# Recurrent steps by token halves, and the final state's product shared by all tiles

## The chip, the cores and the metric

The kernel runs on one core of one Trainium2 chip. The metric is the device time of one execution in microseconds, the median of several. The engines are named as the profile names them: PE is TensorE (PEld its weight loads), ACT is ScalarE, DVE is VectorE, POOL is GpSimd and SP the engine that issues most DMAs.

## The reference, cut to what matters

Eight tiles `t` of 512 tokens with 128 features each pass linear attention (per tile alone), a first layer norm, a recurrence over the tiles, and a second layer norm. The recurrence is where the change lies: token `n` of tile `t` follows token `n` of tile `t - 1`, so tokens don't depend on one another, and only the state of the last tile enters the output.

```
x = layernorm(x + attention(x))                 # tile by tile
def step(c, xt):
    ft = sigmoid(xt @ wf.T + c @ uf.T + bf)
    it = sigmoid(xt @ wi.T + c @ ui.T + bi)
    gt = tanh(xt @ wc.T + c @ uc.T + bc)
    return ft * c + it * gt, None
c_final, _ = lax.scan(step, c0, x)              # over the 8 tiles
h = tanh(einsum('tbi,oi->tbo', x, wo) + c_final @ uo.T + bo)
x = layernorm(x + h)
```

The product `c_final @ uo.T + bo` is the same for all eight tiles.

## The kernel before

Everything stays on the chip. The constants are `T = 8` tiles, `N = 512` tokens and `D = 128` features; a tile has `C = 4` blocks of 128 tokens, and one PSUM bank holds one tile. There is no planner: each engine has its own program, whose order is written out by hand, and engines meet at semaphores. Each engine's queue runs in the order of its program.

The body runs in periods (`periods()`, L197). In period `n` tile `n + 1` has its keys and queries made (`k`), tile `n` its attention products (`a`), tile `n - 1` its attention end and first norm (`b`), and tile `n - 2` its recurrent step (`t`). A step on TensorE is nine products of 512 columns from x1 and nine from the state: weights and operands are each split in a high and a low part in fp32r, and three of the four products are made, for three gates (`gate_x_high` L362, `gate_x_low` L373, `gate_s` L394). ScalarE makes three tanh of a whole bank (`tanh` L545); VectorE makes the kept part (L701), the new part (L774) and the state (L781); ScalarE copies the state's high part (`s_hi`, L591); GpSimd makes the low part (`s_lo`, L276), and VectorE that of the last step (L735). The first norm's result is transposed (`x1_turned` L350), split by ScalarE (`x1_high` L564) and VectorE (`x1_low` L690), and kept as columns (`x1_whole` L568). Only for the last tile are the tanh of gate c, the new part and the state made in two halves.

The output is made in nine parts (`OUT_PARTS`, L148) of a tile each, tile 0 in two. `out_x` (L398) makes x1 times wo, block by block in fp32, and adds the bias; three of the parts come ahead of the last gates on TensorE. `out_s` (L429) adds the last state times uo, again for every block of every tile. Then ScalarE takes the tanh in place (L615), VectorE adds the residual (L790), makes statistics (L663) and variance (L669, L810), GpSimd makes the reciprocal root (L247) and the shift (L255), and of a unit's four blocks VectorE normalises one (L799) and ScalarE three (L557); SP stores the unit (L221). `UNITS` (L46) are seven tiles and the last tile in two halves. ScalarE makes the tanh of unit `u` before it normalises unit `u - ACT_AHEAD`, three earlier; on VectorE a residual stands one unit ahead of the statistics.

## Time and profile before

| | us |
|---|---|
| median of 3 runs | 106.99 |
| lowest, highest | 106.97, 107.19 |
| the profiled execution | 107.27 |
| its span, first to last instruction | 105.2 |

| engine | busy us | share of the span |
|---|---|---|
| TensorE | 92.5 | 88% |
| VectorE | 79.5 | 76% |
| ScalarE | 62.1 | 59% |
| GpSimd | 40.6 | 39% |

The profile comes from one execution, whose time is 2.1 us more than its span. Times inside it count from the span's start. A share of busy time is a mean over stages that have different limits, so the stages have to be read apart. "Chain" is the chain of work that ended last: for each piece the view goes back to what released it. In its rows a TensorE product is set down by its end; in the timeline its row begins where it starts and lasts until its result is written, so products overlap there.

### The profile page before, as it was taken

The page shows a single profiled execution, that of the slowest core. Times are in us where ns is not written, and L with a number is a line of the kernel's source. Part 1 is how long each engine was busy: PE and PEld are TensorE (multiplying, and loading weights), DVE is VectorE, ACT ScalarE, POOL GpSimd, SP SyncE. Part 2 cuts the span into 40 slices and gives each one's busy share as a digit, 9 for nine tenths or more (in the row PEclk, how much of TensorE's full clock was granted, in tenths as well). Part 3 has the DMA queues.
Part 4 walks back from the last instruction along what each step waited for, and adds up shares of the span by engine and source line. Part 5 has one row for each costly group of instructions (what it writes and reads, how often), then busy time and mean ns, then how long its engine had stood idle before and what let it go on. Part 6 is the DMA issues. An engine that isn't in the chain of part 4 may idle for free.

```text
span 105.2 us, 1758 instructions
## 1 busy us (share of the span) xinstructions
PE 92.5 (88%) x570; PEld 78.5 (75%) x570; DVE 79.5 (76%) x225; ACT 62.1 (59%) x115; POOL 40.6 (39%) x59
## 2 busy tenths in 40 slices
PE   6998999889999999999999999999999999991000
PEld 4878779469688968878887888898898899991000
DVE  3325398998999995898689589389592648999950
ACT  1326675349395684676659374374753735799731
POOL 2006277607247149009306604304300002786780
PEclk9999999999999999999999999999999999999855
DMA  1869994000000000000000000000000000034453
GB/s 44 284 250 406 387 386 176 6 0 3 0 0 0 0 0 0 9 0 0 0 0 6 0 0 0 0 0 0 3 0 6 0 0 0 0 142 161 179 211 108
DMA packets 4372, 7.28 MB, mean 69 GB/s; under 512 B 491, under 2 KB 1292, under 8 KB 4364
## 3 DMA queue, kind: packets, MB, share of 16 engines
q1 hardware_dynamic: 3932, 6.85, 17.7%
q10 hardware_dynamic: 432, 0.33, 1.1%
q8 instruction: 4, 0.07, 0.2%
q14 instruction: 4, 0.03, 0.1%
HBM read 5.08 MB, written 2.10 MB: 68 GB/s over the span
## 4 chain that ended last, share of the span: by engine, by line
PE 72%; DVE 18%; POOL 3%; ACT 3%; issue 2%; POOLq 0%; DVEq 0%; ACTq 0%
PE ps_ctx L326 7%; PE ps_k L307 7%; PE ps_ctx L346 6%; PE ps_q L317 5%; DVE stats L663 5%; DVE x L790 4%; PE ps_f L296 4%; PE ps_x L357 3%; POOL rstd L247 2%; DVE x L675 2%; PE ps_f L370 2%; PE ps_f L376 2%; PE ps_c L371 2%; PE ps_c L370 2%; PE ps_c L376 2%; PE ps_i L371 2%
## 5 line engine op out<-in xcount | busy, mean ns | idle before, releaser
L247 POOL TENSOR_TENSOR rstd<-var_eps,minus_half 128x4 f32<-128x4 f32 (+1 forms) x17 | 17.2, 1012 | 22.6 <-DVE var_eps L669 22.3
L276 POOL TENSOR_TENSOR s_lo<-s,s_hi 128x512 fp32r<-128x512 f32 x6 | 7.7, 1291 | 26.7 <-ACT s_hi L591 26.7
L663 DVE BATCH_NORM_STATS2 stats<-x 128x6 f32<-128x256 f32 x32 | 12.3, 425 | 0.3
L675 DVE TENSOR_SCALAR x<-x,stats,rstd 128x128 f32<-128x128 f32 x32 | 11.4, 420 | 0.0
L557 ACT ACTIVATE x<-x,shift,rstd 128x128 f32<-128x128 f32 x21 | 8.9, 480 | 3.6 <-POOL shift L255 3.6
L238 POOL TENSOR_TENSOR k_pair<-k_rows 128x256 f32<-128x256 f32 x8 | 6.3, 785 | 9.9 <-DVE k_rows L697 9.9
L566 ACT ACTIVATE x_hi<-ps_x 128x512 fp32r<-128x512 f32 x8 | 4.8, 597 | 8.6 <-PE ps_x L357 8.6
L326 PEld LDWEIGHTS ps_ctx<-k_rows,x_rows 128*128 128x128 f32 x64 | 8.1, 191 | 2.0 <-issue 1.6
L326 PE MATMUL ps_ctx<-k_rows,x_rows 128*128 128x128 f32 x64 | 8.6, 278 | 0.8 <-DVE x L686 0.5
L307 PE MATMUL ps_k<-wkq,x_cols 128*128 128x128 f32 x64 | 9.3, 293 | 0.0
L537 ACT ACTIVATE k_exp<-ps_k,minus_one 128x512 f32<-128x512 f32 x8 | 5.5, 686 | 6.2 <-PE ps_k L311 6.2
L686 DVE SCALAR_TENSOR_TENSOR x<-ps_ctx,z_inv,x_rows 128x128 f32<-128x128 f32 x32 | 9.0, 341 | 0.1
L346 PEld LDWEIGHTS ps_ctx<-kvo,q_cols 128*128 128x128 f32 x64 | 8.3, 191 | 1.0 <-issue 0.5
L307 PEld LDWEIGHTS ps_k<-wkq,x_cols 128*128 128x128 f32 x64 | 8.8, 209 | 0.2
L346 PE MATMUL ps_ctx<-kvo,q_cols 128*128 128x129 f32 x64 | 8.5, 276 | 0.0
L551 ACT ACTIVATE th_f<-ps_f,half_b 128x512 f32<-128x512 f32 x7 | 4.8, 690 | 5.7 <-PE ps_f L392 5.7
L317 PE MATMUL ps_q<-x_cols,wkq 128*128 128x512 f32 x16 | 8.2, 593 | 0.0
L721 DVE TENSOR_TENSOR kvo<-ps_ctx,eps_z 128x129 f32<-128x129 f32 x8 | 2.3, 293 | 7.5 <-PE ps_ctx L337 7.5
L707 DVE SCALAR_TENSOR_TENSOR keep<-th_f,s 128x512 f32<-128x512 f32 x7 | 4.8, 686 | 3.5 <-ACT th_f L551 3.5
L697 DVE SCALAR_TENSOR_TENSOR k_rows<-k_exp,ps_k 128x512 f32<-128x512 f32 x8 | 5.4, 679 | 1.8 <-ACT k_exp L537 1.8
L774 DVE SCALAR_TENSOR_TENSOR new<-th_i,th_c 128x512 f32<-128x512 f32 (+1 forms) x9 | 5.6, 628 | 1.6 <-ACT th_c L551 1.6
L551 ACT ACTIVATE th_i<-ps_i,half_b 128x512 f32<-128x512 f32 x7 | 4.8, 688 | 2.3 <-PE ps_i L392 2.3
(161 smaller groups left out, 242.2 us busy)
## 6 DMA issues: line engine op xcount, KB each, us to landing
x_cols<-xt SPq DMA_DIRECT2D x8, 256.0 KB, 7.0
x_rows<-x SPq DMA_DIRECT2D x8, 256.0 KB, 7.2
out<-x SPq DMA_DIRECT2D x7, 256.0 KB, 2.0
wgate<-w_gate SPq DMA_DIRECT2D x1, 384.0 KB, 6.7
out<-x SPq DMA_DIRECT2D x2, 128.0 KB, 1.8
wkq<-w_kq ACTq DMA_DIRECT2D x1, 131.0 KB, 3.4
wvo_in<-w_vo_in ACTq DMA_DIRECT2D x1, 128.0 KB, 3.3
wout<-w_out SPq DMA_DIRECT2D x1, 128.0 KB, 6.9
```

The costliest lines, as they stand in the source:

```text
L238: nc.gpsimd.tensor_tensor(k_pair[:], k_rows[:, a % 2, 0:C // 2], k_rows[:, a % 2, C // 2:C], ALU.add).then_inc(k_pair_ok, 1)
L247: nc.gpsimd.tensor_tensor(rstd[:, t, c0:c1], var_eps[:, t, c0:c1], minus_half[:, c0:c1], ALU.pow).then_inc(rstd_ok, 1)
L276: nc.gpsimd.tensor_tensor(s_lo[:, (t - 1) % 2], s[:, (t - 1) % 2].rearrange("p c d -> p (c d)"), s_hi[:, (t - 1) % 2].bitcast(F32), ALU.su ...
L307: nc.tensor.matmul(ps_k[:, c * D:(c + 1) * D], x_cols[:, a, c], wkq[:, WK_T * D:(WK_T + 1) * D], start=(c == 0), stop=False, skip_group_ch ...
L317: nc.tensor.matmul(ps_q[:], wkq[:, WQ_T * D:(WQ_T + 1) * D], x_cols[:, a].rearrange("p c d -> p (c d)"), start=True, stop=True).then_inc(q ...
L326: mm = nc.tensor.matmul(small[:, 0:D], x_rows[:, a, c], k_rows[:, a % 2, c], start=(c == 0), stop=(c == C - 1))
L346: mm = nc.tensor.matmul(ctx_view[:, c // 2, c % 2], q_cols[:, b % 2, c], kvo[:, b % 2], start=True, stop=True, skip_group_check=True)
L551: nc.scalar.activation(out_tile[:, part], ps[:, part], ACT.Tanh, bias=bias, scale=scale).then_inc(ok, 1)
L557: nc.scalar.activation(x1[:, t, c], x1[:, t, c], ACT.Identity, bias=shift[:, t, c:c + 1], scale=rstd[:, T + t, c:c + 1]).then_inc(y2_act_o ...
L663: st = nc.vector.bn_stats(stats[:, t, c:c + 2].rearrange("p c m -> p (c m)"), tile[:, c:c + 2].rearrange("p c d -> p d c"))
L675: nc.vector.tensor_scalar(x1[:, b, c], x1[:, b, c], mean_of(b, c), rstd[:, b, c:c + 1], ALU.subtract, ALU.mult).then_inc(x1_ok, 1)
L686: ins = nc.vector.scalar_tensor_tensor(x1[:, b, c], ctx_view[:, c // 2, c % 2, 0:D], z_inv[:, b % 2, c:c + 1], x_rows[:, b, c, 0:D], ALU.m ...
```

## The change

Steps 0 to 3 are made as before, but steps 4 to 7 are made for tokens 0 to 255 and for tokens 256 to 511 apart, in an order written out in `STEPS`: 4a, 5a, 4b, 6a, 7a, 5b, 6b, 7b (a the first half, b the second), so that with steps 0 to 3 there are twelve entries. The periods end with n = 6, and what follows is written out on each engine. An output unit is now two blocks of two tiles: four units of the first halves, three of the second halves, and the second halves of tiles 6 and 7 alone. For each half the state's product with uo and the bias is made once (`out_g`), split in a high part (ScalarE, `g_high`) and a low part (VectorE, `g_low`), and added to seven of the nine units by two fp32r products with the identity (`add_g`); units 0 and 4 (`DIRECT`) still make the product themselves. The x1 parts have eight buffers instead of two. The low part of the state is made by GpSimd for entries up to 7 and by VectorE for entries 9 and 10. In the tail ScalarE makes the tanh of unit `u` and then normalises unit `u - 1`; VectorE makes residual, statistics and variance of one unit in a row, then its block of the unit before.

```diff
-ACT_AHEAD = 3
-UNITS = [(t, 0, C) for t in range(T - 1)] + [(T - 1, 0, C // 2), (T - 1, C // 2, C)]
-DVE_NORM = [1, 1, 1, 1, 1, 1, 2, 2, 1]
+H = C // 2
+STEPS = [(0, 0, C), (1, 0, C), (2, 0, C), (3, 0, C), (4, 0, H), (5, 0, H), (4, H, C), (6, 0, H),
+         (7, 0, H), (5, H, C), (6, H, C), (7, H, C)]
+FULL_PERIODS = 7
+UNITS = [(0, 2, 0), (2, 2, 0), (4, 2, 0), (6, 2, 0), (0, 2, H), (2, 2, H), (4, 2, H), (6, 1, H), (7, 1, H)]
+DVE_NORM = [1, 1, 1, 1, 1, 1, 1, 1, 1]
+DIRECT = (0, 4)
...
+        g_bank = [ps_x1[:, 0:H * D], ps_q[:, 0:H * D]]
+        unit_bank = [ps_k[:], ps_q[:], ps_ctx[:, 0, :], ps_ctx[:, 1, :], ps_x1[:], ps_k[:], ps_f[:], ps_i[:], ps_c[:]]
...
+            state_low(4)
+            reciprocal_root(6)
+            reciprocal_root(7)
+            state_low(5)
+            state_low(6)
+            state_low(7)
+            for u in range(len(UNITS)):
+                second_root(u)
                 second_shift(u)
...
+            def gate_s(g, k):
+
+                ps, _, done = gates[g]
+                u, last, part = GATES + g, (STEPS[k][0] - 1) % 2, columns(k)
+                if k == 1:
                     pe.wait_ge(split_s_lo, 1)
+                pe.wait_ge(shi_ok[step_before(k)], 1)
+                nc.tensor.matmul(ps[:, part], wgate_hi[:, u], s_hi[:, last, part], start=False, stop=False,
+                                 skip_group_check=True)
...
+            def out_g(h):
+
+                ps = g_bank[h]
+                if h == 0:
                     pe.wait_ge(x1c_ok, T)
+                else:
                     pe.wait_ge(w_ok, 2)
+                pe.wait_ge(uo_ok, 1)
+                pe.wait_ge(s_ok, len(STEPS) if h else STEPS.index((T - 1, 0, H)) + 1)
+                for j in range(H):
+                    nc.tensor.matmul(ps[:, j * D:(j + 1) * D], s[:, (T - 1) % 2, h * H + j], uo_half[:],
+                                     start=(j == 0), stop=False, skip_group_check=True)
+                nc.tensor.matmul(ps, ones_r[:], row_parts[:, BOUT_ROW].unsqueeze(1).to_broadcast([D, H, D]),
+                                 start=False, stop=True, skip_group_check=True).then_inc(g_mm, 1)
+
+            def add_g(u):
+
+                ps, nt, h = unit_bank[u], UNITS[u][1], UNITS[u][2] // H
+                if u == 1:
+                    pe.wait_ge(ident_r_ok, 1)
+                pe.wait_ge(g_hi_ok, h + 1)
+                nc.tensor.matmul(ps[:, 0:nt * H * D], ident_r[:],
+                                 g_hi[:, h].unsqueeze(1).to_broadcast([D, nt, H * D]),
                                  start=False, stop=False, skip_group_check=True)
...
+                pe.wait_ge(g_lo_ok, h + 1)
+                nc.tensor.matmul(ps[:, 0:nt * H * D], ident_r[:],
+                                 g_lo[:, h].unsqueeze(1).to_broadcast([D, nt, H * D]),
+                                 start=False, stop=True, skip_group_check=True).then_inc(out_mm, 1)
...
+            gates_x(5)
+            keys_x(7)
+            gate_s(0, 5)
+            key_values(7)
+            gate_s(1, 5)
+            gate_s(2, 5)
+            context(7)
+            gates_x(6)
+            gates_s(6)
+            x1_turned(6)
+
+            out_x(0)
+            gates_x(7)
+            gates_s(7)
+            x1_turned(7)
             out_x(1)
-            out_x(5)
-            for o in range(len(OUT_PARTS)):
-                if o >= 6:
-                    out_x(o)
-                out_s(o)
+
+            gates_x(8)
+            gates_s(8)
+            gates_x(9)
+            gates_s(9)
+            out_g(0)
+            out_s(0)
+            add_g(1)
+            gates_x(10)
+            out_x(2)
+            gates_s(10)
+            add_g(2)
+            gates_x(11)
+            out_x(3)
+            gates_s(11)
+            add_g(3)
+            out_x(4)
+            out_s(4)
+            out_g(1)
+            for u in range(5, len(UNITS)):
+                out_x(u)
+                add_g(u)
...
+            act.wait_ge(ident_ok, 1)
+            nc.scalar.activation(ident_r[:], ident[:], ACT.Copy).then_inc(ident_r_ok, 1)
...
+            state_high(4)
+            x1_whole(5)
+            xk_copy(7)
+            gates_tanh(5)
+            gates_tanh(6)
+            x1_high(6)
+
+            state_high(5)
+            x1_whole(6)
+            gates_tanh(7)
+            state_high(6)
+            x1_high(7)
+
+            state_high(7)
+            x1_whole(7)
+            gates_tanh(8)
+            gates_tanh(9)
+            g_high(0)
+            out_tanh(0)
+            state_high(9)
+            out_tanh(1)
+            gates_tanh(10)
+            normalise(0)
+            state_high(10)
+            out_tanh(2)
+            normalise(1)
+            gates_tanh(11)
+            out_tanh(3)
+            normalise(2)
+            out_tanh(4)
+            g_high(1)
+            normalise(3)
+            for u in range(5, len(UNITS)):
+                out_tanh(u)
+                normalise(u - 1)
+            normalise(len(UNITS) - 1)
...
+            attention_end(6)
+            key_values(7)
+            normalise(6)
+            kept_state(5)
+            new_state(5)
+            reciprocal_z(7)
+            next_state(5)
+            attention_end(7)
+            step(6)
+            x1_low(6)
+
+            normalise(7)
+            step(7)
+            x1_low(7)
...
+            step(8)
+            step(9)
+            g_low(0)
             second_residual(0)
+            second_statistics(0)
+            second_variance(0)
+            state_low(9)
             second_residual(1)
+            second_statistics(1)
+            second_variance(1)
+            step(10)
+            second_normalise(0)
+            state_low(10)
+            second_residual(2)
+            second_statistics(2)
+            second_variance(2)
+            second_normalise(1)
+            step(11)
+            second_residual(3)
+            second_statistics(3)
+            second_variance(3)
+            second_normalise(2)
+            second_residual(4)
+            g_low(1)
+            second_statistics(4)
+            second_variance(4)
+            second_normalise(3)
+            for u in range(5, len(UNITS)):
+                second_residual(u)
                 second_statistics(u)
                 second_variance(u)
+                second_normalise(u - 1)
             second_normalise(len(UNITS) - 1)
```

## Rows read from the trace of the kernel before

**Rows 1.** The chain's share of the span by engine, from the page.

```profile
PE 72%; DVE 18%; POOL 3%; ACT 3%; issue 2%; POOLq 0%; DVEq 0%; ACTq 0%
```

**Rows 2.** Busy time by stage: stretch, length, busy us (x instructions) by engine, clock.

```profile
62.00:70.30 8.30, 8.09 (x53) 7.03 (x52) 6.38 (x18) 4.13 (x7) 2.31 (x2) 1.00 0.00 0
70.30:78.00 7.70, 7.70 (x50) 6.77 (x49) 6.46 (x18) 4.46 (x7) 2.30 (x2) 1.00 0.00 1
78.00:84.40 6.40, 6.24 (x35) 5.10 (x34) 3.34 (x8) 3.42 (x6) 0.00 (x0) 1.00 0.01 3
...
91.50:105.20 13.70, 3.66 (x31) 3.39 (x29) 9.88 (x40) 9.16 (x22) 8.33 (x15) 0.77 0.42 154
```

**Rows 3.** The chain in order of time: start, duration, engine, tile, line, instructions.

```profile
62.00 0.45 PE ps_x L357 x4
62.47 0.61 ACT x_hi L566
63.21 0.47 PE ps_f L370
63.68 0.24 PE ps_f L371
...
70.31 0.89 PE ps_q L423 x8
...
84.41 0.68 PE ps_k L437 x4
...
102.50 0.49 ACT x L557
```

**Rows 4.** Instruction groups by form: shapes and count, then busy us, mean ns, idle before.

```profile
L238 POOL TENSOR_TENSOR k_pair<-k_rows 128x256 f32<-128x256 f32 x8 | 6.3, 785 | 9.9 <-DVE k_rows L697 9.9
...
L551 ACT ACTIVATE th_c<-ps_c,wkq 128x256 f32<-128x256 f32 x2 | 0.8, 471 | 0.0
...
L781 DVE SCALAR_TENSOR_TENSOR s<-keep,new 128x256 f32<-128x256 f32 x2 | 0.8, 416 | 0.0
```

**Rows 5.** The timeline from 82 to 84.6 us: start, duration, engine, line, operation.

```profile
82.39 0.60 PE L423 MATMUL ps_f<-wout,x_cols 128*128 128x128 f32 x4
...
82.72 0.19 PEld L425 LDWEIGHTS ps_f<-row_parts,ones_r 128*128 128x128 f32 x1
82.75 0.36 PE L425 MATMUL ps_f<-row_parts,ones_r 128*128 128x256 f32 x1
...
82.95 1.06 PE L423 MATMUL ps_x<-wout,x_cols 128*128 128x128 f32 x8
...
83.84 0.75 DVE L781 SCALAR_TENSOR_TENSOR s<-keep,new 128x256 f32<-128x256 f32 x2
```

**Rows 6.** The timeline of the tail, from 86.4 us.

```profile
86.47 0.58 ACT L615 ACTIVATE ps_q<-ps_q 128x512 f32<-128x512 f32 x1 [0.53 <-PE ps_q L437]
87.08 0.69 DVE L790 TENSOR_TENSOR x<-x,ps_q 128x512 f32<-128x512 f32 x1 [0.69 <-ACT ps_q L615]
...
88.48 0.17 DVE L669 TENSOR_SCALAR var_eps<-stats 128x4 f32<-128x4 f32 x1
...
88.73 1.01 POOL L247 TENSOR_TENSOR rstd<-var_eps,minus_half 128x4 f32<-128x4 f32 x1 [13.69 <-DVE var_eps L669]
...
89.88 0.20 POOL L255 TENSOR_TENSOR shift<-minus_mean,rstd 128x4 f32<-128x4 f32 x1
...
90.11 1.26 ACT L557 ACTIVATE x<-x,shift,rstd 128x128 f32<-128x128 f32 x3 [1.27 <-POOL shift L255]
...
94.61 0.57 ACT L615 ACTIVATE ps_i<-ps_i 128x512 f32<-128x512 f32 x1
...
95.12 1.24 ACT L557 ACTIVATE x<-x,shift,rstd 128x128 f32<-128x128 f32 x3
...
96.27 0.57 ACT L615 ACTIVATE ps_c<-ps_c 128x512 f32<-128x512 f32 x1
...
101.23 0.80 POOL L247 TENSOR_TENSOR rstd<-var_eps,minus_half 128x2 f32<-128x2 f32 x1
```

More of the change, by code:

```diff
@@ L187, in rows_of, with columns, step_before, state @@
             return dram[t].rearrange("(p c) d -> p c d", c=C)
-        def halves(cut):
-            return [slice(0, N // 2), slice(N // 2, N)] if cut else [slice(0, N)]
-        def act_norms(units):
-            return sum(c1 - c0 - mine for (_, c0, c1), mine in zip(UNITS[:units], DVE_NORM))
-        def periods():
-            def inside(v):
-                return v if 0 <= v < T else None
-            for n in range(T + 2):
-                yield inside(n + 1), inside(n), inside(n - 1), inside(n - 2)
+        def columns(k):
+            _, c0, c1 = STEPS[k]
+            return slice(c0 * D, c1 * D)
+        def step_before(k):
+            t, c0, _ = STEPS[k]
+            return max(j for j in range(k) if STEPS[j][0] == t - 1 and STEPS[j][1] <= c0 < STEPS[j][2])
+        def state(t):
+            return s[:, t % 2].rearrange("p c d -> p (c d)")
+        def blocks(u):
+            t0, nt, c0 = UNITS[u]
+            return [(t, c) for t in range(t0, t0 + nt) for c in (c0, c0 + 1)]
+        def part_of(tile, u, t_first=0):
+            t0, nt, c0 = UNITS[u]
+            return tile[:, t_first + t0:t_first + t0 + nt, c0:c0 + H]
+        def periods():
+            for n in range(FULL_PERIODS):
+                yield n + 1, n, n - 1 if n >= 1 else None, n - 2 if n >= 2 else None
+        def act_norms(units):
+            return sum(len(blocks(u)) - DVE_NORM[u] for u in range(units))
         @block.sync
@@ new lines, in out_x @@
+                for j, (t, c) in enumerate(blocks(u)):
+                    nc.tensor.matmul(ps[:, j * D:(j + 1) * D], x1_cols[:, t, c], wout[:, 0],
+                                     start=(j == 0), stop=False, skip_group_check=True)
+                n = len(blocks(u))
+                if u not in DIRECT:
+                    return
+                nc.tensor.matmul(ps[:, 0:n * D], ones_r[:], row_parts[:, BOUT_ROW].unsqueeze(1).to_broadcast([D, n, D]),
+                                 start=False, stop=False, skip_group_check=True)
@@ new lines, in out_s @@
+            def out_s(u):
+                ps = unit_bank[u]
+                if u == 0:
+                    pe.wait_ge(uo_ok, 1)
+                pe.wait_ge(s_ok, len(STEPS) if UNITS[u][2] else STEPS.index((T - 1, 0, H)) + 1)
+                n = len(blocks(u))
+                for j, (_, c) in enumerate(blocks(u)):
+                    mm = nc.tensor.matmul(ps[:, j * D:(j + 1) * D], s[:, (T - 1) % 2, c], uo_half[:],
+                                          start=False, stop=(j == n - 1), skip_group_check=True)
+                mm.then_inc(out_mm, 1)
@@ L494, in _ @@
                 if t is not None:
-                    for g in range(GATES):
-                        gate_x_high(g, t)
-                    for g in range(GATES):
-                        gate_x_low(g, t)
-                    if a is not None:
-                        keys_x(a)
+                    gates_x(t)
+                    keys_x(a)
                     gate_s(0, t)
-                if a is not None:
-                    key_values(a)
+                key_values(a)
                 if a == 1:
@@ L767, in _ @@
                 if t is not None:
-                    if t != T - 2:
-                        kept_state(t)
-                    dve.wait_ge(i_ok, t + 1)
-                    parts = halves(t == T - 1)
-                    for h, part in enumerate(parts):
-                        dve.wait_ge(c_ok, t + 1 + h)
-                        nc.vector.scalar_tensor_tensor(new[:, part], th_i[:, part], 1.0, th_c[:, part],
-                                                       ALU.add, ALU.mult).then_inc(new_ok, 1)
@@ L776, in _ @@
-                    if a is not None:
-                        reciprocal_z(a)
-                    dve.wait_ge(keep_ok, t + 1)
-                    for h, part in enumerate(parts):
-                        dve.wait_ge(new_ok, t + 1 + h)
-                        nc.vector.scalar_tensor_tensor(s[:, t % 2].rearrange("p c d -> p (c d)")[:, part], keep[:, part], 0.5,
-                                                       new[:, part], ALU.mult, ALU.add).then_inc(s_ok, 1)
-                if b is not None and b >= 1:
-                    x1_low(b)
```

371 lines of the change are left out of this document (196 added, 175 removed).

## The prediction

> **What bounds the kernel now.** Read the chain by engine first: TensorE holds 72% of it, VectorE 18% [rows 1]. That mean hides two stages, which the busy time by stage parts [rows 2]. Up to 84.4 us TensorE is nearly full (8.09 of 8.30, 7.70 of 7.70, 6.24 of 6.40 us) and everything else waits for it. Behind it the second normalisation runs: TensorE falls to 3.66 us of the last 13.7, and a unit of four blocks moves through ScalarE, VectorE, GpSimd and ScalarE again. The last state is whole at 84.6 us (L781) [rows 5]; from there the chain has 18.4 us to the end of the last ScalarE instruction (103.0 us) [rows 3], and 2.2 more to the end of the span for the last store. So two numbers decide: when the last state stands, and how long the tail behind it is. The change shortens the second (four of nine units come before) and puts work ahead of the first.
>
> **The price of one instruction.** A 512-column gate product takes 0.234 us of TensorE (0.23 and 0.24 in the chain) [rows 3]. A 256-column one isn't in the gates of before, but its like stands once between fp32 products: from the first start (82.39) to the next behind it (82.95) is 0.56 us [rows 5], and the four before it take half of the 0.89 of eight [rows 3], so it takes 0.11. I take 0.117, half of 0.234; the far end is 0.19, the recorded time of a weight load [rows 5], if loads stopped hiding behind so short a product; below 0.107 nothing points. A 256-wide operation takes 0.42 us on VectorE (0.34 where two follow each other), 0.47 (0.37) for ScalarE's tanh, about 0.78 on GpSimd (L238, the nearest row) [rows 4, 5]. From the end of one to the start of the next: 0.04 from TensorE to ScalarE, 0.03 to 0.1 between ScalarE and VectorE and inside VectorE. A TensorE that stood still gives its first 512-column product 0.60 us after the signal (x_hi ends at 63.08, product at 63.68) [rows 3]; for 256 columns 0.49.
>
> **The change, by parts.** (1) Eight half steps for four whole ones: 144 products of 0.117 for 72 of 0.234, nothing on TensorE. On ScalarE and VectorE two halves cost 0.06 to 0.15 us more than a whole, for about 28 pairs some 3 us, mostly beside TensorE; where not, it is in the walk. (2) Product with uo: before, 32 blocks of 0.223 and biases worth eight of 0.235, 9.0 us. After: 12 blocks (2.7), biases 0.7, additions of two products by the identity for seven units (2.8): 6.2 us. The 2.8 us saved lie on an engine that runs ahead in the tail, and are worth nothing there. (3) Order: what else stands on TensorE ahead of the last gate. Before, 10 blocks of x1 times wo with bias, 2.8 us; after, 16 blocks with one bias (3.8), g of the first half (0.56), unit 0's product (0.89), two additions (0.94), 6.2 us. So 3.4 us more ahead of the last state. (4) Copies of g, high and low, 0.4 each on ScalarE and VectorE, twice. (5) One copy of the identity at the start, in ScalarE's wait for the first x·k product: nothing; 0.4 at most if that cover is gone. (6) Eight x1 parts instead of two: no time. (7) State_low of entries 9 and 10 goes to VectorE, queued behind a unit's variance: in the walk. (8) Stores on SP: nine as before, four of them before the last state; nothing else stands on that queue by then, and the last is half a tile as before.
>
> **Walk to the last state.** I laid each engine's new order along these prices, from 53.6 us, where period 6 begins and nothing differs yet. Period 6 has only half of step 4 and ends at 60.6 where it ended at 62.45 [rows 3]. From there TensorE has 24.0 us of work to the end of the last gate (seven half steps of 2.11; attention 2.2; transposes 0.9; the 6.2 of part 3): 84.65 if nothing stops it. It is stopped:
> - 1.0 at gates_x(5), for x_hi of tile 5, which ends at 61.24 (0.6 at that place before).
> - 0.26 at keys_x(7) and key_values(7): less work stands between them and what they wait for.
> - 1.1 at the low products of gates_x(7). VectorE ends s of entry 5 at 67.46, then attention_end(7) to 69.4 (residual 1.1, statistics 0.8), step(6) with its dependent state to 70.7, and only then x1_low(6), 71.34. TensorE is there at 70.6; first low product at 71.83.
> - 0.46 at gates_x(8): x1_high(7) stands on ScalarE behind the three tanh of entry 7 and state_high(6), and ends at 74.53. 0.2 at gates_s(8), for state_low(7) on GpSimd.
> - 0.6 at add_g(1): g is made at 79.87, copied high to 80.3, low on VectorE to 81.25.
> - 0.3 at gates_s(11): state_high(10) stands behind normalise(0) on ScalarE and ends at 86.9, state_low(10) on VectorE at 87.4.
> The sum is 3.95 us: the last gate is ready at 88.6. Its three tanh wait on ScalarE for normalise(1), to 88.5, and the last ends at 89.74, not 89.1. New part (0.10 + 0.42) and state (0.11 + 0.42): 90.8 us, against 84.6.
>
> **Walk of the tail.** One unit, from its rows [rows 6]: tanh to residual 0.61, residual to variance 1.40, variance to root 0.25, root to shift 1.15, shift to ScalarE's normalise 0.23, whose three blocks hold ScalarE 1.15. Before, a residual stands one unit ahead of its statistics; now the statistics wait for their own residual, 0.11 more. So from a unit's tanh to where its normalise lets ScalarE go is 4.90 us. Before, ScalarE had three units of tanh ahead of a normalise, and VectorE set the pace, 1.66 us a unit (tanh at 94.61 and 96.27) [rows 6]. The new order is tanh(u), normalise(u-1), tanh(u+1), normalise(u), so tanh(u+2) stands behind normalise(u): two units per 4.90 us, 2.45 each, with ScalarE idle for the shift. From the last state: unit 4's product and its signal 1.26 (the first four took 0.68 [rows 3]); tanh(4) to tanh(6) 4.90 + 0.25 for g_low(1) between; tanh(6) to tanh(8) 4.90; the last half unit 3.3 (0.4 to its residual, 0.9 to its variance, 0.25 to the root, 1.27 from root to normalise and 0.49 for it, as the last of before [rows 3, 6]); the store 2.2. That is 16.8, against 20.6 before: 3.8 gained.
>
> So the span is 90.8 + 16.8 = 107.6, which is 2.4 over 105.2. The profiled execution took 107.27 us: 109.7. The median of the runs stands 0.28 below it: 109.4 us.
>
> ScalarE keeps its written order in the rows (tanh 94.61, normalise 95.12, tanh 96.27) [rows 6]. The Trainium skill says the same, "TensorE: Matmul & The Clock Gate", section "Architectural detail: the array is 16× 32×32, not 1× 128×128": ScalarE's and VectorE's queues are strict first in, first out. It speaks against this change; without it rival (b) would hold.
>
> **Rivals.** (a) Most of TensorE's stops aren't there, since the halves cover each other better than my walk has it. For: the work alone ends at 84.65, and VectorE has 1.2 to 3 us free in each stage up to 84.4 [rows 2]. Against: each stop is an instruction behind others in its own queue. If those at gates_x(7), gates_x(8), add_g(1) and gates_s(11) and the late tanh go (3.1), the state stands at 87.7, the span is 104.5, the time 106.3; with half of the rest gone too, 105. Below 88.4 for the state the change is faster than before; that is the point from which it decides. 105.7, faster. (b) ScalarE's order costs nothing in the tail and VectorE paces it, 1.8 a unit and 1.15 for each of the two last halves: the last residual starts at 99.6 and not at 102.5, 106.5. Only if normalise is ready much sooner than the rows have it. (c) The narrow products don't hide their weight loads: 0.19 for 0.117, 144 of them, up to 10 us, of which the stops hide up to 3: 114 to 119. Against it is the 0.11 measured once; but that one had fp32 neighbours. (d) The change doesn't do what it says: nothing for it, the first half's units do come before the last state in every queue.
>
> **How the numbers follow.** The walk 0.67 (its own range 107.6 to 111.3: 0.2 on each of ten waits, 0.7 on the tail), (a) 0.20, (b) 0.06, (c) 0.07. The range, 105.8 to 111.3, leaves out (c) and about half of (a). A measurement of this kernel tells 0.2% (0.2 us) from no change. (a) and most of (b) are faster: 0.24. The same 0.04, slower 0.72.
>
> **What the profile of after would show.** Right: the last state near 90.8; TensorE idle about 1 us for x_lo ahead of the low products of gates_x(7); in the tail every second tanh 4.9 us apart and ScalarE waiting for GpSimd's shift; narrow products 0.117 apart. Wrong: the last state before 88.4, tanh of full units 1.8 us apart, or narrow products at 0.13 and more. The likeliest error is a wait put on the wrong engine between 70 and 88 us.

## The result, and the profile after

| | before | after |
|---|---|---|
| median, us | 106.98 | 109.72 |
| lowest, highest | 106.46, 107.19 | 109.29, 110.38 |
| the profiled execution | 107.27 | 109.29 |
| its span | 105.2 | 107.5 |

The ratio of after to before is 1.027, with a 95% interval of 1.021 to 1.033. In a second comparison, beside the experiments, it was 1.031 (1.026 to 1.037). The change makes the kernel 2.7 to 3.1% slower.

The chain by engine (page of after): TensorE has 58% where it had 72%, VectorE 23%, and ScalarE 9% where it had 3% [rows 1].

```profile
PE 58%; DVE 23%; ACT 9%; issue 4%; POOL 3%; POOLq 0%; DVEq 0%; ACTq 0%
```

Busy time by stage of after (stretch, length, then busy us of PE, PEld, DVE, ACT, POOL, and the granted clock). The third stretch ends with the last state, the fourth is the tail:

```profile
60.50:68.60 8.10, 7.95 (x65) 7.71 (x66) 7.01 (x26) 4.08 (x10) 1.75 (x2) 1.00 0.01 2
...
68.60:79.00 10.40, 9.62 (x73) 8.81 (x73) 6.38 (x17) 5.97 (x15) 3.27 (x4) 1.00 0.01 2
...
79.00:90.45 11.45, 10.58 (x81) 9.61 (x80) 10.11 (x30) 8.45 (x21) 4.13 (x6) 1.00 0.10 33
...
90.45:105.30 14.85, 6.06 (x45) 5.42 (x45) 10.90 (x37) 9.63 (x23) 7.37 (x13) 0.81 0.32 109
```

TensorE is no longer nearly full ahead of the last state: 9.62 of 10.40 us and 10.58 of 11.45, against 7.70 of 7.70 [rows 2]. VectorE is busy for 10.11 of the 11.45 us ahead of it.

Executions differ by up to 1 us in where the first periods stand. So I measure from the start of the state of step 3, the last one that all kernels here share, to the end of the last state (**head**), and from there to the end of the span (**tail**).

| kernel | step 3's state starts | last state ends | head | tail |
|---|---|---|---|---|
| before | 53.90 | 84.59 | 30.7 | 20.6 |
| after | 52.95 | 90.45 | 37.5 | 17.05 |
| after, second time | 53.86 | 91.31 | 37.45 | 17.0 |

The head is 6.8 us longer and the tail 3.6 us shorter: 3.25 us, of which the execution shown gave back 0.95 by starting its periods earlier.

The timeline of after at the low products of gates_x(7), at the first products of gates_x(8) and gates_x(9), at add_g(1), and at the last state (start, duration, engine, line, operation):

```profile
69.82 0.68 DVE L834 TENSOR_TENSOR x_lo<-ps_x,x_hi 128x512 fp32r<-128x512 f32 x1
...
70.56 0.39 PE L420 MATMUL ps_f<-x_lo,wgate_hi 128*128 128x256 f32 x1 [0.48 <-DVE x_lo L834]
...
72.52 1.06 PE L474 MATMUL ps_q<-wout,x_cols 128*128 128x128 f32 x8
...
72.97 0.60 ACT L683 ACTIVATE x_hi<-ps_x 128x512 fp32r<-128x512 f32 x1
...
73.72 0.36 PE L411 MATMUL ps_f<-x_hi,wgate_hi 128*128 128x256 f32 x1
...
75.92 0.47 ACT L650 ACTIVATE th_f<-ps_f,half_b 128x256 f32<-128x256 f32 x1 [0.51 <-PE ps_f L443]
...
76.44 0.38 PE L411 MATMUL ps_f<-x_hi,wgate_hi 128*128 128x256 f32 x1
...
76.81 0.39 PE L411 MATMUL ps_i<-x_hi,wgate_hi 128*128 128x256 f32 x1
...
80.61 0.42 DVE L961 TENSOR_TENSOR g_lo<-ps_x,g_hi 128x256 fp32r<-128x256 f32 x1
...
81.08 0.51 PE L519 MATMUL ps_q<-g_lo,ident_r 128*128 128x512 f32 x1 [0.29 <-DVE g_lo L961]
...
88.94 0.46 ACT L650 ACTIVATE th_c<-ps_c,wkq 128x256 f32<-128x256 f32 x1
...
89.11 0.42 DVE L850 SCALAR_TENSOR_TENSOR keep<-th_f,s 128x256 f32<-128x256 f32 x1
...
89.50 0.43 DVE L857 SCALAR_TENSOR_TENSOR new<-th_i,th_c 128x256 f32<-128x256 f32 x1
...
90.03 0.42 DVE L864 SCALAR_TENSOR_TENSOR s<-keep,new 128x256 f32<-128x256 f32 x1
```

TensorE waits for x_lo (0.48 us by the record, 0.75 in lost products) and for g's low part. At gates_x(8) it waits for x_hi of tile 7, though the row names no releaser: x_hi ends at 73.57, the product starts at 73.72, and that is 1.20 us after the eight products of out_x(1) started, where 0.82 us stand between two such starts elsewhere in after (82.48 and 83.30). So 0.4 us is lost there. In gates_x(9) there is a wait that no bullet of the walk has: a gate has one bank, and its next products wait until ScalarE has read the last ones (th_f ends at 76.39, the product starts at 76.44). That makes the three pairs 0.37 us apart for 0.24 (76.44, 76.81 and 77.17).

ScalarE's timeline of the tail of after:

```profile
91.72 0.57 ACT L669 ACTIVATE ps_x<-ps_x 128x512 f32<-128x512 f32 x1
...
93.63 1.26 ACT L674 ACTIVATE x<-x,shift,rstd 128x128 f32<-128x128 f32 x3 [0.97 <-POOL shift L287]
...
94.80 0.57 ACT L669 ACTIVATE ps_k<-ps_k 128x512 f32<-128x512 f32 x1
...
95.80 1.26 ACT L674 ACTIVATE x<-x,shift,rstd 128x128 f32<-128x128 f32 x3 [0.43 <-POOL shift L287]
...
96.96 0.57 ACT L669 ACTIVATE ps_f<-ps_f 128x512 f32<-128x512 f32 x1
...
98.66 1.26 ACT L674 ACTIVATE x<-x,shift,rstd 128x128 f32<-128x128 f32 x3 [1.12 <-POOL shift L287]
...
99.82 0.36 ACT L669 ACTIVATE ps_i<-ps_i 128x256 f32<-128x256 f32 x1
...
100.82 1.26 ACT L674 ACTIVATE x<-x,shift,rstd 128x128 f32<-128x128 f32 x3 [0.63 <-POOL shift L287]
...
101.98 0.36 ACT L669 ACTIVATE ps_c<-ps_c 128x256 f32<-128x256 f32 x1
```

The first row is the tanh of unit 4. From 94.80 on each tanh starts as a normalise ends. Tanh of units 4, 6 and 8 stand at 91.72, 96.96 and 101.98, and those of units 5 and 7 at 94.80 and 99.82: two units in 5.0 to 5.2 us. Between tanh and normalise ScalarE waits for GpSimd's shift (1.12 us ahead of 98.66).

### The profile page after: what moved, and what is told of

The parts are those of the page before. It is cut to its first block, busy times and chain, and to the rows that moved or that the text cites. A ratio compares the mean times of both kernels' runs of the same rounds, so it can differ in the third digit from the quotient of the medians.

```text
span 107.5 us, 1913 instructions
## 1 busy us (share of the span) xinstructions
PE 91.6 (85%) x611; PEld 78.8 (73%) x611; DVE 83.3 (77%) x236; ACT 65.2 (61%) x134; POOL 41.8 (39%) x61
## 4 chain that ended last, share of the span: by engine, by line
PE 58%; DVE 23%; ACT 9%; issue 4%; POOL 3%; POOLq 0%; DVEq 0%; ACTq 0%
PE ps_ctx L366 7%; PE ps_k L347 6%; PE ps_ctx L386 5%; PE ps_q L357 5%; ACT x L674 4%; PE ps_f L336 3%; DVE stats L974 3%; DVE x L817 3%; DVE x L966 3%; POOL rstd L280 3%; DVE s L864 2%; PE ps_x L397 2%; PE ps_ctx L376 2%; PE ps_f L420 2%; DVE new L857 2%
## 5 line engine op out<-in xcount | busy, mean ns | idle before, releaser
L293 POOL TENSOR_TENSOR s_lo<-s,s_hi 128x512 fp32r<-128x512 f32 (+1 forms) x8 | 8.1, 1010 | 23.2 <-ACT s_hi L660 23.2
L280 POOL TENSOR_TENSOR rstd<-var_eps,minus_half 128x4 f32<-128x4 f32 (+1 forms) x9 | 9.5, 1054 | 16.2 <-DVE var_eps L982 16.2
L674 ACT ACTIVATE x<-x,shift,rstd 128x128 f32<-128x128 f32 x23 | 9.8, 485 | 5.8 <-POOL shift L287 5.8
L275 POOL TENSOR_TENSOR rstd<-var_eps,minus_half 128x4 f32<-128x4 f32 x8 | 8.7, 1084 | 11.6 <-DVE var_eps L811 11.3
L650 ACT ACTIVATE th_f<-ps_f,half_b 128x256 f32<-128x256 f32 (+1 forms) x11 | 5.9, 532 | 7.3 <-PE ps_f L443 7.1
L347 PE MATMUL ps_k<-wkq,x_cols 128*128 128x128 f32 x64 | 8.4, 275 | 0.0
L850 DVE SCALAR_TENSOR_TENSOR keep<-th_f,s 128x256 f32<-128x256 f32 (+1 forms) x11 | 5.4, 490 | 3.0 <-ACT th_f L650 3.0
L650 ACT ACTIVATE th_i<-ps_i,half_b 128x256 f32<-128x256 f32 (+1 forms) x11 | 5.8, 528 | 2.7 <-PE ps_i L443 2.7
L857 DVE SCALAR_TENSOR_TENSOR new<-th_i,th_c 128x256 f32<-128x256 f32 (+1 forms) x12 | 6.1, 511 | 1.7 <-ACT th_c L650 1.7
L864 DVE SCALAR_TENSOR_TENSOR s<-keep,new 128x256 f32<-128x256 f32 (+1 forms) x12 | 6.5, 542 | 0.7
```

The costliest lines, as they stand in the source:

```text
L275: nc.gpsimd.tensor_tensor(rstd[:, b], var_eps[:, b], minus_half[:], ALU.pow).then_inc(rstd_ok, 1)
L280: nc.gpsimd.tensor_tensor(part_of(rstd, u, T), part_of(var_eps, u, T), minus_half[:, 0:nt * H].rearrange("p (t c) -> p t c", c=H), ALU.pow ...
L347: nc.tensor.matmul(ps_k[:, c * D:(c + 1) * D], x_cols[:, a, c], wkq[:, WK_T * D:(WK_T + 1) * D], start=(c == 0), stop=False, skip_group_ch ...
L650: nc.scalar.activation(out_tile[:, part], ps[:, part], ACT.Tanh, bias=bias, scale=scale).then_inc(ok, 1)
L674: nc.scalar.activation(x1[:, t, c], x1[:, t, c], ACT.Identity, bias=shift[:, t, c:c + 1], scale=rstd[:, T + t, c:c + 1]).then_inc(y2_act_o ...
L857: nc.vector.scalar_tensor_tensor(new[:, part], th_i[:, part], 1.0, th_c[:, part], ALU.add, ALU.mult).then_inc(new_ok, 1)
```

## The experiments

The ratio is to runs of the kernel before on the same chip. Head and tail are as above.

| kernel | us | ratio (95%) | head | tail |
|---|---|---|---|---|
| after again | 109.72 | 1.031 (1.026 to 1.037) | 37.45 | 17.0 |
| e1, tanh two units ahead | 106.52 | 1.003 (0.999 to 1.007) | 37.5 | 14.4 |
| e2, no shared product | 108.84 | 1.020 (1.014 to 1.026) | 37.0 | 16.8 |
| e3, before with shared product | 106.95 | 1.005 (1.001 to 1.009) | 30.6 | 21.5 |
| e4, before with ACT_AHEAD 2 | 111.20 | 1.041 (1.035 to 1.047) | 30.7 | 25.4 |
| e5, queue order | 109.17 | 1.026 (1.022 to 1.031) | 37.2 | 17.1 |
| e6, e1 and e5 | 106.54 | 1.002 (0.999 to 1.005) | 37.2 | 14.35 |
| e7, e6 and VectorE's tail | 106.52 | 1.003 (1.000 to 1.006) | 37.1 | 14.2 |
| e8, e1 with units 2, 3 behind | 108.60 | 1.018 (1.013 to 1.023) | 36.9 | 16.7 |
| e9, e7 with VectorE freed | 105.77 | 0.992 (0.988 to 0.995) | 36.4 | 14.2 |
| e10, e9 with norms moved | 105.84 | 0.993 (0.990 to 0.996) | 36.4 | 14.5 |
| e11, e1 with all units behind | 110.70 | 1.039 (1.030 to 1.048) | 35.1 | 20.4 |

The kernel before had medians of 106.32 to 106.51 us beside them.

**The changed kernel again**, unedited, as the measure for the others:

> The changed kernel as it is, as the base for the three beside it on the same chip: 2.7% over the kernel before, the last state at 90.2 to 90.5 us of the span.

Measured: 109.72 us, 1.031 (1.026 to 1.037), head and tail as in the first execution to 0.1 us. The last state ends at 91.31 and not at 90.2 to 90.5, since the periods of this execution stand 0.9 us later.

### The tail: ScalarE's order

**e1**, on the changed kernel:

```diff
             out_tanh(4)
             g_high(1)
-            normalise(3)
             for u in range(5, len(UNITS)):
                 out_tanh(u)
-                normalise(u - 1)
+                normalise(u - 2)
+            normalise(len(UNITS) - 2)
             normalise(len(UNITS) - 1)
```

> The changed kernel, with only ScalarE's order in the tail altered: tanh(5) to tanh(8) each stand ahead of normalise(3) to normalise(6), that is, tanh runs two units ahead of normalise and not one. Theory 1 (the tail is paced by tanh(u+2) standing behind normalise(u), 2.5 us a unit): the pace falls to VectorE's 1.8 us a unit, the last unit's residual starts near 99.6 and not at 102.4, the time is about 2.8 us shorter, 106.9 (106.2 to 107.6). The last state stays at 90.4. Rival (the tail is paced by VectorE or by GpSimd's root and shift, ScalarE's order only follows): within 0.5 us of the changed kernel, 109.2 to 109.8.

Measured: 106.52 us, 1.003. The head is the same to 0.1 us, the tail 2.7 us shorter. The timeline of e1 at ScalarE's tanh and VectorE's residuals:

```profile
93.83 0.58 ACT L669 ACTIVATE ps_k<-ps_k 128x512 f32<-128x512 f32 x1 [1.28 <-PE ps_k L519]
...
94.44 0.69 DVE L966 TENSOR_TENSOR x<-x,ps_k 128x512 f32<-128x512 f32 x1
...
95.48 0.58 ACT L669 ACTIVATE ps_f<-ps_f 128x512 f32<-128x512 f32 x1
...
96.37 0.68 DVE L966 TENSOR_TENSOR x<-x,ps_f 128x512 f32<-128x512 f32 x1
...
97.14 0.37 ACT L669 ACTIVATE ps_i<-ps_i 128x256 f32<-128x256 f32 x1
...
98.28 0.41 DVE L966 TENSOR_TENSOR x<-x,ps_i 128x256 f32<-128x256 f32 x1
```

Tanh of units 5, 6 and 7 are now 1.65 us apart, for 2.5 in after, and VectorE paces: its residuals stand 1.92 us apart (94.44, 96.37, 98.28), with its other work between them. The pace was expected at 1.8. Theory 1 is shown, its rival is out.

**e4**, on the kernel before, where the same loop is made by one number:

```diff
-ACT_AHEAD = 3
+ACT_AHEAD = 2
```

> The kernel before, with ACT_AHEAD 2 in place of 3: tanh runs two units ahead of normalise; there a residual stands one unit ahead of its statistics, so this makes the same loop as the changed kernel's (tanh(u+3) behind normalise(u), whose statistics need tanh(u+1)): two units per 4.8 us. Theory 1: from tanh of tile 3 on, 2.4 us a unit for 1.66; about 4.6 us slower, 111.6 (110.8 to 112.4). Rival (VectorE paces whatever ScalarE's order): within 0.5 us of before.

Measured: 111.20 us, 1.041, 4.9 us over the median beside it, where 4.6 were expected. ScalarE's timeline of e4:

```profile
90.78 0.57 ACT L615 ACTIVATE ps_ctx<-ps_ctx 128x512 f32<-128x512 f32 x1
...
92.45 0.57 ACT L615 ACTIVATE ps_x<-ps_x 128x512 f32<-128x512 f32 x1
...
94.53 1.26 ACT L557 ACTIVATE x<-x,shift,rstd 128x128 f32<-128x128 f32 x3 [1.51 <-POOL shift L255]
...
95.70 0.57 ACT L615 ACTIVATE ps_f<-ps_f 128x512 f32<-128x512 f32 x1
```

Two tanh 1.67 us apart, then 3.25: two units in 4.92 us, with ScalarE idle 1.51 us for the shift ahead of 94.53. The order alone makes that wait, in either kernel.

### The shared product

**e2**, on the changed kernel:

```diff
-DIRECT = (0, 4)
+DIRECT = tuple(range(9))
...
-            out_g(0)
             out_s(0)
-            add_g(1)
+            out_s(1)
...
-                add_g(u)
+                out_s(u)
```

> The changed kernel without the shared product: every unit makes its own product with uo and its bias, so g, its two copies and the identity products are gone; halves and order stay. Theory 1 (the shared product saves TensorE time where it is not needed): ahead of the last state TensorE has 0.75 us more work but does not wait about 0.5 us for the low part of g, in the tail 0.25 us between residual and statistics go: 109.4, within 0.4 of the changed kernel. Rival (the shared product carries the change, and the loss would be larger without it): the last state comes 0.8 us later and the tail is TensorE's, 110.5 or more. Rival 2 (the waits for g are what costs): faster by over 0.5 us.

Measured: 108.84, 1.020 (1.014 to 1.026), where after has 1.027 and 1.031: 0.7 to 1.1% under it. The head is 0.5 us shorter and the tail 0.2. Expected was no change within 0.4, which failed; rival 2 (faster by over 0.5 us) fits better. But e2 takes away the waits for g and the copies of g on ScalarE and VectorE together, so it is not shown which of them costs. The interval of e2 overlaps that of the first comparison of after (1.021 to 1.033) and ends where that of the second begins (1.026), so the size is not settled.

**e3**, on the kernel before (tiles 3 to 7 by identity products from one g of 512 columns):

```diff
+                if o == 4:
+                    out_g()
+                    out_x(6)
...
+                if o >= 4:
+                    add_g(o)
+                else:
+                    out_s(o)
```

> The kernel before, with only the shared product: whole steps, old units, but for tiles 3 to 7 the product with uo and the bias is made once (512 columns, bank of tile 7), split and added by identity products. TensorE has about 2.1 us less work. Theory 1 (worth nothing, since VectorE paces that tail): VectorE has 0.69 us more, and tile 3's product waits for the low part of g until about 90.5: 0.7 to 1.0 us slower, 107.8. Rival (TensorE's saving counts): faster than before by 0.5 us or more.

Measured: 106.95, 1.005 (1.001 to 1.009), 0.6 us over before where 0.7 to 1.0 was expected. Counted from the state of step 3, TensorE's last product ends 1.15 us sooner, and nothing comes of it: g's low part keeps tile 3's tanh back to 89.44, and VectorE has 0.69 us more. The head is 0.1 us shorter since a bias product of tile 3 left it. The shared product is no gain in either kernel.

### Ahead of the last state

**e5**, on the changed kernel, order only:

```diff
             attention_end(7)
-            step(6)
             x1_low(6)
+            step(6)
...
             gates_tanh(7)
-            state_high(6)
             x1_high(7)
+            state_high(6)
...
             out_s(0)
-            add_g(1)
             gates_x(10)
+            add_g(1)
...
-            normalise(1)
             gates_tanh(11)
             out_tanh(3)
-            normalise(2)
+            normalise(1)
             out_tanh(4)
             g_high(1)
+            normalise(2)
             normalise(3)
```

> The changed kernel with the order in the queues altered ahead of the last state, nothing added or removed: x1_low(6) ahead of step(6) on VectorE; x1_high(7) ahead of state_high(6) and the tanh of entry 11 and of unit 3 ahead of normalise(1), and tanh(4) ahead of normalise(2), on ScalarE; add_g(1) behind gates_x(10) on TensorE. The tail's order from unit 5 on stays. Theory 1 (the late last state is made of single instructions that stand behind others): the stop at gates_x(7) loses 0.5 to 0.9 us, that at gates_x(8) 0.4, at add_g(1) 0.3, and the tanh of entry 11 come 0.5 sooner; some of it comes back elsewhere: last state 1.5 us earlier, 88.9, and 1.5 us off the changed kernel's time (1.2 to 2.0). Rival (TensorE and the recurrence's own chain fill that time, the stops only show their slack): under 0.5 us.

Measured: 109.17, 0.55 us under the changed kernel beside it, the head 0.3 us shorter. Theory 1 wanted 1.2 to 2.0 us and falls for its size; the head fits the rival's bound of 0.5, the time is just over it. The stops were there, and changing the order at them gave little, because the ones looked at here had another wait behind them. The timeline of e5, at gates_x(7) and at the last state:

```profile
70.23 0.83 POOL L293 TENSOR_TENSOR s_lo<-s,s_hi 128x256 fp32r<-128x256 f32 x1
...
70.38 0.96 DVE L857 SCALAR_TENSOR_TENSOR new<-th_i,th_c 128x256 f32<-128x256 f32 x1
...
71.78 1.11 DVE L817 TENSOR_SCALAR x<-x,stats,rstd 128x128 f32<-128x128 f32 x4
...
88.56 0.47 ACT L650 ACTIVATE th_c<-ps_c,wkq 128x256 f32<-128x256 f32 x1
...
89.69 0.41 DVE L857 SCALAR_TENSOR_TENSOR new<-th_i,th_c 128x256 f32<-128x256 f32 x1
```

With x1_low(6) first, step(6) meets GpSimd's state_low(5) (its new part takes 0.96 us), normalise(7) ends at 72.9, and the transposes of tile 7 wait where the low products had waited: they start 0.84 us ahead of out_x(1) (72.27 and 73.11), for 0.44 in after (72.08 and 72.52). TensorE's stop has moved by some instructions. At the end the last tanh of entry 11 ends at 89.03, but the kept part starts at 89.35 and the new part at 89.69, behind unit 2's residual, statistics and variance on VectorE. In after tanh and VectorE's queue came free within 0.1 us of one another: th_c ends at 89.40, and the new part starts at 89.50, behind a kept part that starts at 89.11. So the earlier tanh of e5 gives nothing by itself.

**e6**, e5's order with e1's:

> The queue order of e5 and tanh two units ahead of normalise as in e1. If the two causes are apart (one ahead of the last state, one behind it), their gains add: 1.5 + 2.7 = 4.2 us off the changed kernel, 1.4% under the kernel before (0.980 to 0.991). If both free the same time: no more than the larger of the two, about the kernel before.

Measured: 106.54, 1.002 (0.999 to 1.005), outside the expected 0.980 to 0.991. By head and tail the gains add (0.3 and 2.7 us), but there was only 0.3 us of the first. In the time that 0.3 can't be told from e1's 1.003.

**e7**, e6 with VectorE's order in the tail:

```diff
-            second_normalise(2)
             second_residual(4)
             g_low(1)
+            second_normalise(2)
             second_statistics(4)
             second_variance(4)
-            second_normalise(3)
             for u in range(5, len(UNITS)):
                 second_residual(u)
+                second_normalise(u - 2)
                 second_statistics(u)
                 second_variance(u)
-                second_normalise(u - 1)
+            second_normalise(len(UNITS) - 2)
             second_normalise(len(UNITS) - 1)
```

> e6, and on VectorE in the tail normalise(u-2) stands between residual(u) and statistics(u), so that statistics don't wait for their own residual and normalise never waits for the root. Theory 1 (VectorE paces this tail once ScalarE doesn't, 1.92 us a unit in e1): 0.1 us a unit for five units, 0.4 to 0.5 us under e6. Rival (the pace is then TensorE's or the latency of the last unit): the same as e6.

Measured: 106.52, 1.003, the tail 0.1 us shorter where 0.4 to 0.5 was expected: within the noise of e6. The pace on VectorE fell from 1.92 to 1.81 us a unit, and the last residual stands 0.3 us nearer to the last state than in e1 (9.0 and 9.3 us behind its end), but half of that is lost again: the last unit's statistics now stand behind a block of the unit before (0.59 us from residual to statistics for 0.45).

**e8**, on e1, units 2 and 3 behind the last gates in every queue (TensorE's shown):

```diff
             gates_x(10)
-            out_x(2)
             gates_s(10)
-            add_g(2)
             gates_x(11)
-            out_x(3)
             gates_s(11)
+            out_x(2)
+            add_g(2)
+            out_x(3)
             add_g(3)
```

> The kernel of e1, with units 2 and 3 (out_x, add_g and all that follows on ScalarE and VectorE) moved behind the last gates in every queue; compare it with e1. Theory 1 (work put ahead of the last gate costs its own length there): 2.25 us of products leave TensorE's queue there and the last state comes 2.2 us earlier. Theory 2 (that work fills time in which the half steps would wait for one another): with it gone TensorE waits for the low part of the state, and the last state comes 1.0 us earlier at most (28.9 us behind the state of step 4's first half, for 29.9), while VectorE gets two more units behind it: 0.5 to 1.5 us slower than e1. Theory 1 with VectorE's pace of 1.8 a unit: about e1, within 0.5.

Measured: 108.60, 1.018, 1.6 us over e1 by the two ratios, 0.1 over theory 2's range. For 2.25 us of products taken away the head is 0.6 us shorter, and the tail is 2.3 us longer. TensorE's timeline of e8 shows where the rest went:

```profile
83.76 0.39 PE L443 MATMUL ps_f<-s_lo,wgate_hi 128*128 128x256 f32 x1 [0.49 <-DVE s_lo L875]
...
87.08 0.39 PE L438 MATMUL ps_f<-s_hi,wgate_hi 128*128 128x256 f32 x1 [0.77 <-ACT s_hi L660]
```

It stands idle for the low part and then for the high part of the state (1.26 us in all), and the first products of gates_x(11) wait for their banks, as those of gates_x(9) do (0.36 us a pair from 84.72).

**e11**, on e1, g and units 0 to 3 behind:

```diff
             gates_s(9)
-            out_g(0)
-            out_s(0)
-            add_g(1)
             gates_x(10)
-            out_x(2)
             gates_s(10)
-            add_g(2)
             gates_x(11)
-            out_x(3)
             gates_s(11)
+            out_g(0)
+            out_s(0)
+            add_g(1)
+            out_x(2)
+            add_g(2)
+            out_x(3)
             add_g(3)
```

> The kernel of e1, with g of the first half and units 0 to 3 all moved behind the last gates, in every queue; only x1 times wo of units 0 and 1 stays ahead. It measures what the half steps cost alone. 4.9 us of products and additions leave TensorE's queue ahead of the last gate, 4.0 us of unit work VectorE's. Theory 2 (the last steps 6b and 7b stand alone, and one half step alone needs about 3.65 us from state to state, as 7b in e8): the last state 27.5 us behind the state of step 4's first half, for 29.9 in e1, that is 2.4 earlier for 4.9 us of work; nine units behind it at 1.9 us: 111.5 to 112.5. Theory 1 (work ahead of the last gate costs its length): the state 4.5 to 5 us earlier, 109.5 to 110.5.

Measured: the last state starts 27.46 us behind that of step 4's first half (29.9 in e1), as theory 2 had it; the time, 110.70 (1.039), lies between the two ranges and doesn't decide: 0.8 us under theory 2's, whose tail was costed too long, and 0.2 over theory 1's. The timeline of e11:

```profile
83.95 0.42 DVE L864 SCALAR_TENSOR_TENSOR s<-keep,new 128x256 f32<-128x256 f32 x1
...
84.41 0.42 ACT L660 ACTIVATE s_hi<-s 128x256 fp32r<-128x256 f32 x1 [1.09 <-DVE s L864]
...
84.85 0.43 DVE L875 TENSOR_TENSOR s_lo<-s,s_hi 128x256 fp32r<-128x256 f32 x1 [0.48 <-ACT s_hi L660]
...
84.87 0.39 PE L438 MATMUL ps_f<-s_hi,wgate_hi 128*128 128x256 f32 x1 [0.65 <-ACT s_hi L660]
...
87.06 0.43 DVE L857 SCALAR_TENSOR_TENSOR new<-th_i,th_c 128x256 f32<-128x256 f32 x1 [0.37 <-ACT th_c L650]
...
87.59 0.43 DVE L864 SCALAR_TENSOR_TENSOR s<-keep,new 128x256 f32<-128x256 f32 x1
```

From state to state one half step alone takes 3.64 us (83.95 to 87.59): 0.46 until the high part is begun, 0.44 more until the low part and the first product, the nine products, then tanh, new part and state. The nine products start over 1.3 us of it; the rest of the way is other engines'. The work ahead of the last gate had cost 2.4 us. Its products are 4.2 us by the prices of part (3) (g 0.56, unit 0's product 0.89, two additions 0.94, eight blocks 1.78); the expectation's 4.9 is more than they add up to.

And e11 answers what the halves cost without g and the units. On TensorE its head has the same gate products as before and 0.8 us less of other work (8 blocks with one bias, 2.0 us, for 10 with theirs, 2.8), and is 35.1 us for 30.7: **4.4 us for steps 4 to 7 by halves**, in this order of the queues. The other 2.4 us of the 6.8 are the g product and units 0 to 3. How much of the 4.4 another order would give back was not tried on e11; on the kernel with all its work, the orders of e5 and e9 took 1.1 us off the head.

**e9**, e7 with VectorE freed between the steps:

```diff
             state_low(7)
+            state_low(9)
             for u in range(len(UNITS)):
...
             second_variance(0)
-            state_low(9)
...
             step(10)
-            second_normalise(0)
-            state_low(10)
             second_residual(2)
+            state_low(10)
             second_statistics(2)
             second_variance(2)
+            second_normalise(0)
             second_normalise(1)
...
             gates_tanh(10)
-            normalise(0)
-            state_high(10)
             out_tanh(2)
+            state_high(10)
+            normalise(0)
```

> The kernel of e7, with VectorE relieved from 82 to 90 us: state_low(9) goes to GpSimd; tanh of unit 2 stands ahead of state_high(10) and normalise(0) behind it on ScalarE; residual(2) stands ahead of state_low(10) on VectorE, so that it does not idle there. Theory 1 (from g on the last state is paced by VectorE's queue, which has units 0 to 2 between the steps): last state 0.4 to 0.8 us earlier than in e7 (29.56 behind the state of step 4's first half), and as much off the time: 1.0 to 1.5% better than e7 at best, 0.992 to 0.998 of the kernel before. Rival (TensorE's queue paces it): the last state within 0.1 of e7.

Measured: 105.77, 0.992 (0.988 to 0.995), the head 0.8 us shorter than e7's. The timeline of e9, behind the state of entry 9:

```profile
80.27 0.43 DVE L865 SCALAR_TENSOR_TENSOR s<-keep,new 128x256 f32<-128x256 f32 x1
...
81.58 0.73 POOL L293 TENSOR_TENSOR s_lo<-s,s_hi 128x256 fp32r<-128x256 f32 x1 [6.12 <-ACT s_hi L661]
```

The low part starts 1.31 us behind that state; in e7, behind unit 0's variance on VectorE, it started 2.61 us behind (80.98 and 83.59). At entry 11 the kept part starts 0.34 us behind the end of its tanh, for 1.05 in e7. So from g on the last state was held up by VectorE's queue, which had units 0 to 2 between the steps. The three edits were made together, and what each gives is not shown; ScalarE's copy of the high part of entry 10's state stands 0.46 us behind the state in both. This version is faster than both kernels, by 0.7 us (0.8%) against the one before, a small gain but clear of 1 by its interval.

**e10**, e9 with one block of units 2 and 4 moved to ScalarE:

```diff
-DVE_NORM = [1, 1, 1, 1, 1, 1, 1, 1, 1]
+DVE_NORM = [1, 1, 0, 1, 0, 1, 1, 1, 1]
```

> The kernel of e9, with VectorE's block of units 2 and 4 normalised by ScalarE (four blocks there, none on VectorE). If VectorE paces the tail and ScalarE has room: 0.3 to 0.5 us under e9. If ScalarE has none left: the same or slower.

Measured: 105.84, the same as e9. In its trace the four blocks of unit 2 hold ScalarE for 1.64 us, and VectorE's residual of unit 5 waits 0.42 us for a tanh that stands behind them: ScalarE, at 1.65 us a unit in e1, has no room for a fourth block.

## Why the prediction was right, point by point

Predicted were 109.4 us (105.8 to 111.3), slower; measured 109.7.

- **What bounds.** The two numbers, when the last state stands and how long the tail is, did decide. 90.8 was forecast for the first, 90.45 stands in after; 16.8 us for the second, 17.05 measured. The span was to be 107.6 and is 107.5. That is closer than the walk deserves: it began at before's 53.6 us, and after's periods stood 0.95 us earlier. On one base the walk was 0.6 us short for the head (36.9 for 37.5) and 0.25 for the tail. Against the kernel before the forecast was 1.023, and 1.027 and 1.031 were measured: right in direction and size, a little low.
- **The price of a narrow product.** 0.117 was taken; in after, products of 256 columns start 0.12 us apart (the nine products of gates_s(7), with their weight loads, stand at 71.02 to 71.96). Rival (c) is out.
- **The stops.** x_hi of tile 5, x_lo of tile 6, g's low part stand where the walk put them (0.78, 0.48 and 0.29 us by the record). At gates_x(7) the stop costs 0.75 us and not 1.1. At gates_x(8) 0.46 was booked for x_hi of tile 7, and 0.4 is there; x_lo of that tile costs another 0.3, which the walk didn't have. The stop at gates_s(11) is about 0.2 for 0.3. One term was missed, the wait for the bank at gates_x(9): 0.4. The stops add up to 3.92 and not 3.95, which changes nothing.
- **What the stops mean** was wrong. Rival (a) priced five of them at 3.1 us, and the prediction named instructions behind others in a queue as the cause. e5 changed the order at four of the five, 2.8 us by the walk, and took 0.3 us off the head, since other waits stood behind. e9, which relieved VectorE from 82 us on and so also changed what stands ahead of gates_s(11), took off 0.8 more. A walk along queues gives the right time for one order, but the term it books at a wait isn't what taking the wait away gives. (Rival (a)'s further case, "half of the rest gone too", comes to 105.6 us by its own terms and not to 105.)
- **Part (3), 3.4 us more work ahead of the last state**, was right as a sum and wrong as a price: e8 and e11 show that such work costs a quarter to somewhat over half of itself (0.6 of 2.25, 2.4 of 4.2). Part (1), "nothing on TensorE", is true of its products but left the larger cause unnamed: by e11 the halves without that work lengthen the head by 4.4 us. Of the 6.2 us by which the walk lengthened the head, 3.4 were work; of the measured 6.8, the work is 2.4 and the halves are 4.4.
- **The product with uo.** Worth nothing in the tail, as said; e3 and e2, over the whole kernel, show it slightly below nothing.
- **The tail.** The loop of tanh and normalise was put at 5.15 us with g_low(1) in it and at 4.90 without; 5.24 and 5.02 were measured. The 0.1 in each is GpSimd's root (1.10 for 1.01 us [rows 6]), which here runs beside VectorE's block; in e7 and e9, where a residual stands there, it took 1.01. e1 and e4 show the mechanism on both kernels. Rival (b), VectorE's pace, was put at 106.5; e1, which makes it so, took 106.5, and that they agree to the digit is partly luck: beside e1 the kernel before took 106.34, so the forecast ratio was 0.995 and the measured one 1.003, and the tail shrank by 2.7 us where 2.9 was forecast. The rule that the prediction took from the Trainium skill, "TensorE: Matmul & The Clock Gate", section "Architectural detail: the array is 16× 32×32, not 1× 128×128", that ScalarE's and VectorE's queues are strict first in, first out, agrees with ScalarE's rows of after, e1 and e4: in after the tanh at 96.96 starts only behind the normalise of 95.80, and e1, which changes ScalarE's order alone, moves it.

## What to carry to other kernels

Where units pass through several engines with hand-written queues, count how many units an engine's early stage begins before its late stage must finish the first of them. The way round once, divided by that number, is a lower bound on the pace: here 5.0 to 5.2 us by two, since tanh(u+2) stands behind normalise(u), and one more unit ahead was worth 2.7 us of tail. Cutting a recurrent step in halves leaves product time alone but not the way from state to state (two of 3.64 us are 7.3, and the last whole step with all its other work had 6.4 [rows 2]), so the halves pay only where other work fills the gap, and what fills it must not stand ahead of the next step on the engine that makes the state. A wait in a trace is where the next limit shows, not what its removal gives: look for what is ready just behind it before pricing it.

## What the runs showed of the hardware

- VectorE's operations on two SBUF operands stretched where they started 0.1 to 0.25 us behind GpSimd's state_low: the state of 256 columns took 0.76 us (it starts at 73.41, state_low at 73.16) in after and 0.42 elsewhere, and the new part 0.96 in e5 (70.38 and 70.23). One that was under way when state_low began kept its time (the new part at 72.88 in after, 0.43 us), and so did those beside GpSimd's root (the new part at 68.95, 0.42 us, beside the root from 68.74 on). VectorE's operations that read PSUM kept theirs too (the four residuals 1.12 us beside state_low at 61.05, as elsewhere).
- GpSimd's root of 128x4 numbers took 1.10 to 1.19 us where VectorE had begun a block, a kept part or a low part up to 0.17 us ahead of it (94.31 behind the block at 94.21 in after), and 1.01 where a residual had begun there (95.59 behind the one at 95.49 in e9). Both are units of two tiles of two blocks, so the layout is not the reason; the first norm's root of one tile took 1.11 too, behind a kept part (68.74 and 68.57 in after).
- ScalarE's and VectorE's 256-column operations kept the 0.35 to 0.37 and 0.34 us between two starts (71.58 and 71.95 on ScalarE, 65.33 and 65.67 on VectorE, in after) that stood in the trace of before once or twice.
